# Splitting the experts' matrices in DVE's waits, a scan for the running sums, and earlier gathers at the end, in a one-core vision tower

## What is computed

```python
router_logits = jnp.einsum('bsh,he->bse', x, router_w) + router_b      # 8 experts
router_probs = jax.nn.softmax(router_logits, axis=-1)
top_k_probs, top_k_indices = jax.lax.top_k(router_probs, 2)
top_k_probs = top_k_probs / jnp.sum(top_k_probs, axis=-1, keepdims=True)
...
expert_out = jax.nn.gelu(jnp.einsum('bsh,ehd->ebsd', x, expert_w) + expert_b[:, None, None, :])
combined = jnp.einsum('bse,ebsd->bsd', gates, expert_out)
return jnp.einsum('bsd,df->bsf', combined, out_w) + out_b
...
h = h + _L0_ffn_ref(_layernorm(h, axis=-1), ...)
```

## Time and profile before

| | |
|---|---|
| median of 3 runs | 824.71 us (824.49 to 826.41) |
| the profiled execution | 825.01 us |
| its span in the trace | 823.2 us |
| PE busy | 699.2 us, 85% of the span |
| DVE busy | 537.3 us, 65% |
| ACT busy | 405.1 us, 49% |
| POOL busy | 157.6 us, 19% |
| PE's share of the chain that ended last | 64% |
| DVE's share of it | 22% |
| DMA's share of it | 6% |
| moved by DMA | 74.25 MB, 90 GB/s over the span |

### The profile page before, as it was taken

The page is one execution under the profiler, slowest core; times in us unless marked ns, Lnnn a source line. Parts: engine busy times, 40 slices in busy tenths (PEclk is TensorE's granted clock), DMA queues, the critical chain, the costliest instruction groups (busy, mean ns, idle before and its releaser), DMA issues.

```text
span 823.2 us, 16543 instructions
## 1 busy us (share of the span) xinstructions
PE 699.2 (85%) x5638; PEld 555.7 (68%) x5639; DVE 537.3 (65%) x1206; ACT 405.1 (49%) x1056; POOL 157.6 (19%) x282
## 2 busy tenths in 40 slices
PE   4758887879999999999999998775339999992998
PEld 3447877758787777868687785353328888881776
DVE  4998983657677777767677666457965444441765
ACT  4825544577576665757667565414623333330111
POOL 4000001000111102111111101124322323213451
PEclk9979999999999999999999999597559999996999
DMA  7100356200010000001000044142065566546774
GB/s 236 36 0 14 117 133 155 37 1 3 1 52 0 25 25 25 25 13 39 0 25 25 25 179 167 39 171 112 0 217 142 165 162 169 158 147 209 201 211 144
DMA packets 53495, 74.25 MB, mean 90 GB/s; under 512 B 24505, under 2 KB 26809, under 8 KB 53330
## 3 DMA queue, kind: packets, MB, share of 16 engines
q1 hardware_dynamic: 40338, 40.72, 15.2%
q0 software_dynamic: 5920, 19.40, 9.8%
q10 hardware_dynamic: 7200, 13.63, 4.3%
HBM read 45.42 MB, written 28.33 MB: 90 GB/s over the span
## 4 chain that ended last, share of the span: by engine, by line
PE 64%; DVE 22%; DMA 6%; issue 3%; ACT 3%; POOL 1%; SPq 0%; DVEq 0%; ACTq 0%; POOLq 0%
PE ps L1811 39%; PE ps L1914 7%; PE ps L1924 4%; PE ps L1907 4%; DMA rows<-y_slots,slot_of 4%; PE ps L2091 3%; DVE ring L1283 3%; DVE ring L1284 2%; PE ps L1956 2%; PE ps L1758 2%; DVE negmax L1351 2%; DVE ew_lo L1659 1%; DVE of_place L1639 1%; POOL rows L785 1%; DMA b_in<-in_L_tok_B_ri_dram 1%
## 5 line engine op out<-in xcount | busy, mean ns | idle before, releaser
L948 ACT ACTIVATE pts<-ps 128x512 f32<-128x512 f32 x128 | 77.2, 603 | 119.1 <-PE ps L1914 118.9
L940 ACT ACTIVATE prb<-ps,negmax 128x257 f32<-128x257 f32 x256 | 117.9, 479 | 4.5 <-DVE negmax L1351 3.5
L1351 DVE TENSOR_REDUCE negmax<-ps 128x2 f32<-128x514 f32 x128 | 82.5, 686 | 38.3 <-PE ps L1907 38.3
L1914 PE MATMUL ps<-ident,prb 128*128 128x128 f32 x512 | 84.4, 289 | 8.7 <-ACT pts L948 4.2
L1914 PEld LDWEIGHTS ps<-ident,prb 128*128 128x128 f32 x512 | 57.3, 144 | 33.9 <-issue 12.3
L1360 DVE TENSOR_SCALAR prb<-prb,rrec 128x258 f32<-128x258 f32 x256 | 73.4, 352 | 2.3
L1811 PE MATMUL ps<-ew_hi,xnT_hi 128*128 x160 | 66.9, 418 | 1.0 <-DVE xnT_lo L1549 1.0
L1086 ACT ACTIVATE rows<-ps 128x512 f32<-128x512 f32 x40 | 23.9, 598 | 87.7 <-DVE ps L1672 87.7
L1811 PE MATMUL ps<-ew_lo,xnT_hi 128*128 x160 | 63.6, 397 | 0.0
L1811 PE MATMUL ps<-ew_hi,xnT_lo 128*128 x160 | 63.6, 397 | 0.0
L1758 PE MATMUL ps<-ident,ring 128*128 128x128 f32 x384 | 48.2, 282 | 15.5 <-DVE ring L1284 14.4
(11 more groups left out here) (377 smaller groups left out, 1841.4 us busy)
## 6 DMA issues: line engine op xcount, KB each, us to landing
y_slots<-rows ACTq DMA_DIRECT2D x40, 256.0 KB
ew<-in_L_ffn_expert_w_dram SPq DMA_DIRECT2D x8, 1024.0 KB, 8.6
h_dram<-h_ob SPq DMA_DIRECT2D x17, 256.0 KB, 2.0
xn_dram<-tok SPq DMA_DIRECT2D x17, 256.0 KB, 2.2
h_early<-h_dram SPq DMA_DIRECT2D x9, 256.0 KB, 7.3
out_dram<-h_early SPq DMA_DIRECT2D x9, 256.0 KB
tok_dram<-so SPq DMA_DIRECT2D x4, 512.0 KB, 3.4
tok<-tok_dram SPq DMA_DIRECT2D x16, 128.0 KB, 3.0
```

The source lines that it names most:

```text
L940: e = act.activation(prb[:, u % 2, j, 0:KEYS], ps[:, j, 0:KEYS], ACT.Exp, bias=negmax[:, u % 2, j:j + 1], accum_out=rowsum[:, u % 2, j:j + 1])
L948: act.activation(pts[:, slot:slot + 2, :, st * P:(st + 1) * P], ps[:, 4, :].rearrange("p (h t s) -> p h t s", h=2, t=HALVES), ACT.Copy).th ...
L1351: dve.tensor_reduce(negmax[:, u % 2, 2 * b:2 * b + 2], ps[:, 2 * b:2 * b + 2, 0:KEYS], AX_X, ALU.max, negate=True).then_inc(s["dve_max"], 1)
L1914: mm = pe.transpose(ps[:, 4, (2 * j + tt) * P:(2 * j + tt + 1) * P], prb[:, u % 2, 2 * b + j, tt * P:(tt + 1) * P], ident[:, :])
```

## The change

- **Low parts.** POOL makes none. ACT makes the high parts of experts 0 to 2 at the end of attention, of 3 and 4 where 0 and 1 stood, 5 and 6 ahead of `of_tile`, and 7 behind it. DVE makes low parts 0 and 1 ahead of the last batch's first residual, 2 behind that residual's statistics, 3 ahead of reading the tokens' sums, 4 to 6 behind the gates and 7 behind the second slot tile's low part. PE waits, for the first two slot tiles, for the low part of the tile's own expert, and in the loop for all eight.
- **Running sums.** The table of picks is laid out by expert, then column. One scan with a table `inside` (1, and 0 where an expert's columns begin) gives the running sums and, in its last column, the row's count; L1605 and the six steps are gone.
- **Places.** `of_place` is made in four pieces (8, 8, 8 and 10 columns).
- **Output matrix.** Its load also waits for three turned slot tiles, ACT's high part follows the second gelu, and DVE's low part follows the last slot tile's low part. Two tiles of `h` are loaded ahead, the others one by one, each waiting for the combination of tile t - 2.
- **Gathers of the end.** DVE works out how many tiles of slots are used, rounded up to an even number; POOL loads the number and waits for so many stores only, and runs one small operation on `pairs_used` before it gathers. The ring has four tiles. Seven slot tiles that may stay unused are filled with zeros at startup, by seven stores of 256 KB on SP's queue. The first combinations wait for the last turned slot tile instead of the last expert matmul.

The diff, cut to its core:

```diff
             for k in range(SEL):
                 sp.dma_start(y_slots[(SLOTS + k) * P:(SLOTS + k + 1) * P, :], u_sb[:, :]).then_inc(st_h[k], 16)
+            for i in range(USED, SLOTS):
+                sp.dma_start(y_slots[i * P:(i + 1) * P, :], u_sb[:, :]).then_inc(ld_ew[NE - 1], 16)
...
             sp.wait_ge(s["dve_token_of"], 1)
+            sp.wait_ge(s["pe_slot_turned"], 3)
             sp.dma_start(ow[:, :, :], out_w.rearrange("(k p) d -> p k d", p=P)).then_inc(s["loaded_out_w"], 16)
             for t in range(EARLY_H):
-                sp.dma_start(h_early[:, t, :], h_dram[t]).then_inc(s["loaded_h"], 16)
+                sp.dma_start(of_end(t), h_dram[t]).then_inc(s["loaded_h"], 16)
             sp.wait_ge(s["pe_expert"], SLOTS)
-            for t in range(EARLY_H, NT):
-                sp.dma_start(h_late[:, t - EARLY_H, :], h_dram[t]).then_inc(s["loaded_h_late"], 16)
+            def load_h(t):
+                sp.wait_ge(s["dve_combined"], 2 * (t - 1))
+                sp.dma_start(of_end(t), h_dram[t]).then_inc(ld_ew[(t - EARLY_H) % Y_RING], 16)
+            load_h(EARLY_H)
             for t in range(TILES + 1):
+                if EARLY_H < t + 2 < NT:
+                    load_h(t + 2)
                 sp.wait_ge(s["dve_out"], t + 1)
...
-            for table in (chosen, cum_a, cum_b):
-                pool.memset(table[:, 0:PAD, :], 0.0).then_inc(s["pool_sums_cleared"], 1)
-            for e in range(POOL_LOWS):
-                pool.wait_ge(s["act_expert_high"], e + 1)
-                pool.tensor_tensor(ew_lo[:, e, :, :], ew[:, e, :, :], ew_hi[:, e, :, :].bitcast(F32), ALU.subtract
-                                   ).then_inc(s["pool_expert_low"], 1)
+            pool.memset(inside[:, :, :], 1.0).then_inc(s["pool_sums_cleared"], 1)
+            pool.wait_ge(s["pool_sums_cleared"], 2)
+            pool.memset(inside[:, :, 0], 0.0).then_inc(s["pool_sums_cleared"], 1)
...
+            pool.wait_ge(s["dve_stores_used"], 1)
+            stored = pool.value_load(stores_used[0:1, 0:1], min_val=8 * USED, max_val=8 * SLOTS)
             for done in st_y:
-                pool.wait_ge(done, 16 * SLOTS // 2)
+                pool.wait_ge(done, stored)
+            pool.tensor_tensor(pairs_used[:, 1:2], pairs_used[:, 0:1], pairs_used[:, 0:1], ALU.mult)
             for t in range(NT):
-                if t >= 2:
-                    pool.wait_ge(s["dve_combined"], 2 * (t - 1))
+                if t >= Y_RING:
+                    pool.wait_ge(s["dve_combined"], 2 * (t - Y_RING + 1))
...
             keep_pt(last, UNITS - 1, 0)
             keep_pt(last, UNITS - 1, 1)
+            act.wait_ge(s["pe_scores"], NB * UNITS)
+            act.wait_ge(s["pe_cls_scores"], NB)
+            act.wait_ge(s["pe_values"], NB * HALVES)
+            hi_expert(0)
             hi_ot(last, 3)
+            hi_expert(1)
+            act.wait_ge(s["pe_pv"], NB * KC)
+            hi_expert(2)
             act.wait_ge(s["dve_attn_done"], 1)
...
             gelu(1, 1, True)
+            act.wait_ge(s["loaded_out_w"], 16)
+            act.activation(ow_hi[:, :, :], ow[:, :, :], ACT.Copy).then_inc(s["act_out_w_high"], 1)
             with act.Fori(1, SLOTS // 2 - 1) as k:
...
+            for e in range(2):
+                lo_expert(e)
             residual(last, 0, 6)
             dve.wait_ge(s["dve_residual"], last * HALVES + 1)
             residual_stats(last, 0)
+            lo_expert(2)
             residual(last, 1, 7)
...
-            dve.tensor_reduce(row_count[:, :], picked.rearrange("p c e -> p e c"), AX_X, ALU.add
-                              ).then_inc(s["dve_row_count"], 1)
+            dve.tensor_tensor_scan(flat(cum), flat(inside), flat(picked), 0.0, ALU.mult, ALU.add
+                                   ).then_inc(s["dve_row_count"], 1)
             dve.tensor_tensor(spread[:, 0, :], top8[:, :, 1], top8[:, :, 0], ALU.subtract).then_inc(s["dve_gate_gap"], 1)
-            level, a, b = 1, chosen, cum_a
-            while level < COLS:
-                then(dve.tensor_tensor(b[:, PAD:, :], a[:, PAD:, :], a[:, PAD - level:PAD - level + COLS, :], ALU.add))
-                level, a, b = 2 * level, b, (cum_b if b is cum_a else cum_a)
...
+            then(dve.tensor_scalar(pairs_used[:, 0:1], tiles_to[:, 1, 3 + NE:4 + NE], 0.5, 0.25, ALU.mult, ALU.add))
+            then(dve.tensor_scalar(pairs_used[:, 1:2], pairs_used[:, 0:1], ROUND_MAGIC, ROUND_MAGIC, ALU.add, ALU.subtract))
+            dve.tensor_scalar(stores_used[:, :], pairs_used[:, 1:2], 16.0, None, ALU.mult).then_inc(s["dve_stores_used"], 1)
+            lo_expert(LOWS_IN_ATTENTION)
             dve.wait_ge(s["pe_token_of"], 1)
...
             lo_xs(1, 1)
+            lo_expert(NE - 1)
             dve.wait_ge(s["loaded_biases"], 16)
             add_bias(0, 0)
-            dve.wait_ge(s["act_out_w_high"], 1)
-            dve.tensor_tensor(ow_lo[:, :, :], ow[:, :, :], ow_hi[:, :, :].bitcast(F32), ALU.subtract
-                              ).then_inc(s["dve_out_w_low"], 1)
...
             def combine(t, u, first):
-                dve.wait_ge(got_y[u], 16 * (t - u) + 32)
+                dve.wait_ge(got_y[t % Y_RING], 32 * (t // Y_RING + 1))
                 if first:
-                    dve.wait_ge(s["pe_expert"], SLOTS)
+                    dve.wait_ge(s["pe_slot_turned"], SLOTS)
...
             def residual_out(t, u):
+                if t >= EARLY_H:
+                    dve.wait_ge(ld_ew[(t - EARLY_H) % Y_RING], 16 * ((t - EARLY_H) // Y_RING + 2))
...
             pe.wait_ge(s["dve_expert_of"], 1)
-            pe.wait_ge(s["dve_expert_low"], NE - POOL_LOWS)
-            pe.wait_ge(s["pool_expert_low"], POOL_LOWS)
```

More of the change, by code:

```diff
@@ L263, in vit_tower_kernel @@
         xnT_lo = sb(ffn, "xnT_lo", [P, 2, KC, P], F32R)
+        combT_hi, combT_lo, comb = xnT_hi, xnT_lo, rows[:, 0:2]
         eb = sb(ffn, "eb", [P, NE, D])
@@ L304, in vit_tower_kernel @@
             "pool_out_bias": "a tile with the output bias added, to be kept for the end",
-            "pool_sums_cleared": "zeros before the running sums",
-            "pool_expert_low": "low part of one of the first experts' matrices",
+            "pool_sums_cleared": "zeros ahead of the tiles' sums, then where the running sums of an expert begin",
             "act_exp_params": "exponentials of the parameters",
@@ L362, in vit_tower_kernel @@
             "dve_logits": "logits of four tiles with the bias",
-            "dve_row_count": "a row's number of entries for each expert",
+            "dve_row_count": "running sums of a row's entries for each expert",
             "dve_gate_gap": "second logits less first ones",
             "dve_hit": "the slots' tiles, one-hot",
-            "dve_onehot": "the slots' tiles times the tokens' tiles, then two pieces of the slots' places, one-hot",
+            "dve_onehot": "the slots' tiles times the tokens' tiles, then pieces of the slots' places, one-hot",
             "dve_token_of": "the token of every slot",
@@ L369, in vit_tower_kernel @@
             "dve_gates": "the gates",
+            "dve_stores_used": "how many stores of slots hold a token's result",
             "dve_expert_low": "low part of an expert's matrix",
@@ L422, in vit_tower_kernel @@
             "loaded_h": "the first token tiles, back for the end",
-            "loaded_h_late": "the other token tiles",
             "stored_xn": "normed token tiles",
@@ L593, in _ @@
                     sp.dma_start(out[:, 0, :], of_end(t)[0:NB]).then_inc(s["stored_out"], 16)
+            for done in st_y:
+                sp.wait_ge(done, 16 * SLOTS // 2)
             sp.wait_ge(s["stored_out"], (TILES + 1) * 16)
@@ L1063, in _ @@
                                ).then_inc(s["act_logitsT_kept"], 1)
-            for e in range(2):
+            for e in range(3, 5):
                 hi_expert(e)
@@ L1621, in _ @@
                                           in1=ps[:, 0, 0:NE], op0=ALU.mult, op1=ALU.add))
[L1622 to L1625 removed]
+            z = inside[:, :, :]
+            then(dve.tensor_tensor(z, cum[:, :, :], bc(first_slot[:, :].unsqueeze(2), [P, NE, COLS]), ALU.add))
+            then(dve.tensor_tensor(z, z, picked[:, :, :], ALU.mult))
+            then(dve.tensor_reduce(slotf[:, :], z.rearrange("p e c -> p c e"), AX_X, ALU.add))
             then(dve.tensor_tensor(slotf[:, COLS - SEL:], slotf[:, COLS - SEL:], spare[:, :], ALU.add))
@@ L1688, in _ @@
             lo_xs(SLOTS - 1, 1)
+            dve.wait_ge(s["act_out_w_high"], 1)
+            dve.tensor_tensor(ow_lo[:, :, :], ow[:, :, :], ow_hi[:, :, :].bitcast(F32), ALU.subtract
+                              ).then_inc(s["dve_out_w_low"], 1)
             add_bias(SLOTS - 2, 0)
@@ L2133, in _ @@
             pe.wait_ge(s["dve_row_count"], 1)
-            pe.matmul(ps[:, 0, 0:NE], before[:, :], row_count[:, :], start=True, stop=True)
-            pe.matmul(ps[:, 1, 0:NE], all_one[:, :], row_count[:, :], start=True, stop=True).then_inc(s["pe_ranks"], 1)
```

(11 more changed lines are left out.)

84 lines of the change are left out of this document (40 added, 44 removed).

## The result

| | before | after |
|---|---|---|
| median, runs side by side | 825.56 us (824.49 to 826.74) | 795.05 us (793.04 to 795.57) |
| the profiled execution | 825.01 us | 795.57 us |
| its span | 823.2 us | 793.6 us |

The ratio is 0.963 (95% interval 0.960 to 0.965): faster, by 30.5 us. The forecast was 791.4 with a range of 787.0 to 799.0. Its span would have been 789.6; the trace shows 793.6, so 4.0 us are to be found. Engine totals first, from the page of the kernel after: busy us and share of the span, then the engines' shares of the chain that ended last.

What follows compares the result with a forecast made beforehand. TensorE was busy 85% of the span, so time could only come from stretches where it waits. 16.2 us surviving to the last expert matmul plus 17.4 in the end stage, 33.6 off 825.01, gave 791.4; range 787.0 to 799.0.

Steps and rivals of the forecast that it cites:

- Routing, 12.0 off: Routing up to `token_of`: without POOL's low parts holding up DVE, `token_of` is there at 585.9 instead of 597.9.
- Low parts and first gathers, 18.4 in all: Between `token_of` and the experts: three low parts and the gathers nearly level, first expert matmul at 593.9 instead of 612.27.
- Attention tail, cost 0: Low parts 0 to 2 fit ACT's and DVE's holes at the end of attention: cost 0, at most 2.6 us.
- Nothing lost ahead of the routing: Startup stores of zeros and parts in attention taken at cost 0; routing starts as before, at 567.5.
- Output matrix, stall 2.2: Ahead of the fourth expert tile: later load and ACT's part stall PE, leaving 16.2 us off; stall bounds 0 to 4.
- Stores 0 to 35 and the meeting of gather and last bias: End stage: POOL waits for 36 tiles' stores; first gathered pair (743.1) meets DVE's last bias (743.06), old clock.
- First projection at the slow price, 5.1: Start of end stage: PE at its slow clock, projection 0 takes 5.1 us, 2.6 less at the fast level.
- Rival 2: PE keeps the 2.4 GHz level at the start of the end stage: 788.8 us, chance 0.20.
- PE sets the pace of the end: End stage: PE's turns and matmuls set 3.20 us a tile instead of 3.66; the stage is 17.4 off.
- rivals 1, 4, 5 and 6: Transfers pace end, 796.7 to 798.3 (0.20); 38 stores, 797.8 (0.05); routing stays long, 799.4 (0.04); transfers slower, 841 (0.03).
- 3: The attention tail or the startup isn't covered: 791.9 to 794.5 us, chance 0.08.

Runs made afterwards that it cites:

- Experiment 1: Changed kernel with POOL making low parts 0 to 2 in the routing again and DVE none in attention: 812.62 us, 13.3 above the changed kernel of its group.
- Experiment 3: Changed kernel with `of_place` in two pieces of 24 and 10 columns instead of four: 799.56 us, 0.3 above the changed kernel of its group.
- Experiment 2: Changed kernel with DVE making low parts 0 to 2 outside the attention tail, part 0 ahead of the tokens, others behind the gates: 806.98 us, 7.7 above its sibling.
- experiment 8: The changed kernel run again unchanged, as sibling of the last group's runs: 798.85 us, ratio 0.966 to the kernel before.
- 11: Changed kernel with the output matrix loaded in four parts and the seven stores of zeros moved later: 794.71 us, against 798.85 for the unchanged sibling.
- experiment 6: Changed kernel with each `h` tile of the end stage loaded a second time into an unused buffer (15 loads, 3.9 MB): 793.96 us, ratio 0.961.
- experiment 7: Changed kernel with ACT's high part of the output matrix eight slot tiles later and DVE's low part moved too, load unmoved: 793.82 us, ratio 0.960.
- Experiment 9: Also "the kernel with quarters": changed kernel, output matrix in four loads behind successive slot turns, `h` loads and ACT's and DVE's parts moved: 795.70 us, sibling 798.85.
- Experiment 4: Changed kernel with POOL waiting for the stores of all 40 slot tiles: 804.79 us, 10.8 above the 793.96 and 793.82 of its group.
- Experiments 5: Changed kernel with end-stage gathers only two tiles ahead instead of four: 800.01 us, 6.1 above the two fastest of its group.
- the three groups: The follow-up runs, each group on one chip beside the kernel before, which took 826.40, 826.75 and 826.48 us.

## Why the prediction was right, and where it was off

- **Routing, 12.0 off: right.** 18.3 us from the comparison to `token_of` (570.53 to 588.80), as forecast (18.36). Experiment 1 shows the reason by undoing it. One reading was loose: the second piece of `of_place` did not end with POOL's third subtraction (593.67) but 1.4 us behind it, at 595.04, its own length; the sum does not use it. The scan, taken at 0.64 between bounds of 0.44 and 2.7, took 0.73. PE was the bound behind the first piece, as said, and experiment 3 shows 2.1 us for the pieces at that place.
- **Low parts and first gathers, 18.4 in all: right to 0.1.** The two gathers and the three low parts were nearly level, as forecast: the gathers' turns wait until 592.89 and 594.84, DVE is free for the first slot low part at 595.91. Experiment 2 gives 6.7 us for three parts.
- **Attention tail, cost 0: right for this profile, and with less room than it seems.** Timeline of the kernel after; the last of these was forecast with its 0.65 beside POOL:

```profile
534.30 4.49 DVE L1543 TENSOR_TENSOR ew_lo<-ew,ew_hi 128x2048 fp32r<-128x2048 f32 x2
538.70 0.68 DVE L1390 TENSOR_TENSOR tok<-ps,tok 128x512 f32<-128x512 f32 x1
540.03 2.87 DVE L1543 TENSOR_TENSOR ew_lo<-ew,ew_hi 128x2048 fp32r<-128x2048 f32 x1
```

  The first residual stands 1.6 later than in the earlier trace rows, but it is not the parts that hold it: everything from 529 on is later by as much, and the chain runs through PE's matmuls there. The holes that the prediction measured were those of a PE at the slow level (the 16 matmuls ahead of `oT_hi` take 1.83 in the chain before and 1.97 after). In two later profiles, those of experiments 8 and 11, the same 16 take 1.08, at the full clock, and the chain goes through the moved parts instead. Chain of experiment 8:

```profile
529.76 1.36 ACT ew_hi L1047
...
533.85 4.40 DVE ew_lo L1543 x2
...
539.59 2.79 DVE ew_lo L1543
```

  ACT's part holds `oT_hi` from about 531.1 to 531.56 there, and DVE's hold the class rows' residual from about 543.9 to 544.28: some 0.8 us in all, an estimate from PE's last matmuls ahead of each (they end at 531.05 and 543.80).
- **Nothing lost ahead of the routing: wrong, by 3.0 in this profile, and for the most part not by the change.** 1.6 us had gathered by the end of attention, 0.3 of them already in a load ahead of every changed instruction (`b_in`, 8.00 against 7.70). The other 1.4 are a clock phase: behind the same wait of 3.35 us in both kernels, the 16 turns at 553.18 took 3.18 at the slow level. The next 16 took 1.90, the first ones of the kernel before 1.90, and those of experiment 6 as well. In the twelve other profiles, of this kernel and its variants, the comparison starts between 566.6 and 569.6, at 568.1 in the mean, where the kernel before has 567.5 and the kernel after 570.5: the profile after is the latest of all. The prediction took the trace of before as the common start of both sums and had no term for such phases; the range had to hold them, and did.
- **Output matrix, stall 2.2: mis-sized.** The time from the first to the fourth expert tile was 14.95 us against 14.55 (+0.4), but a term was missing: PE's clock behind the stop, +1.75. And the mechanism was only half of it. The step said issue to use, then ACT, then DVE; experiment 7 took ACT and DVE out and a stop of 1.98 stayed, because the loads issued beside it (1 MB of the matrix and 0.5 MB of `h`) also delay the fifth tile's gather. Experiment 9 spread them and the stop was gone.
- **Stores 0 to 35 and the meeting of gather and last bias: right, to 0.4.** The chain leads from the bias of tile 35 at 718.65 over its store to POOL at 724.00, and the first combination at 731.56 follows the last bias (730.95) without a wait; tile 1's waits 0.37. Experiment 4 prices the early start at 9 to 11 us.
- **First projection at the slow price, 5.1: mis-sized.** It took 3.86; the clock came back in its midst. Rival 2 took 2.6 off, so the truth lay between the two (in the terms of the chain, the kernel before had 4.82 for this projection, and a fast one takes 2.8). In experiment 7 it took 4.60, and in the kernel with quarters the whole first 10 us are slow. Which of these comes can't be read from the trace of before.
- **PE sets the pace of the end: right.** 3.23 a tile against 3.20, PE 20.00 of 20 us. Experiments 5 and 6 bound it on both sides: with two tiles of ring gathers pace it, with four there is room for 3.9 MB more. The likeliest case was the one that came; rivals 1, 4, 5 and 6 fell, 2 was half right, and 3 came closest to the time (791.9 to 794.5) with a reason that the runs don't bear out in this profile. That the total came within 3.7 us is in part luck: the slow clock behind the stop (+1.75) and the first projection (-1.6 with what is ahead of it) are errors of opposite sign, and on two other chips the same kernel took 799.

## What to carry to other kernels

Before moving elementwise work to GpSimd, look at what VectorE does at the same time: a POOL subtraction over 2048 elements made operations of 0.44 and 0.72 us take 4.7 to 4.9. Work placed in VectorE's own waits cost nothing while TensorE was the slower, and 0.8 us where TensorE happened to run at its full clock: measure such holes at both levels. A large load needed late is best cut into pieces, each behind one step of the loop, since it delays the small gathers beside it as well as its own consumer. A stop of 3 to 4 us cost TensorE more than its length (1.75 us on top in the kernel after, 2.7 in experiment 6), one of 2.0 did not. A DMA share near 1.0 is no proof of a limit: add a load and see whether the time moves.

## What the runs showed of the hardware that was not expected

- The DMA engines moved 407 GB/s of gathers, loads and stores over 20 us (experiment 6), above the 393 of the earlier trace rows; the share there reads 1.04 and was 0.98 at 339, so it does not tell what is left.
- A gather's issue on POOL takes 0.94 to 0.95 us alone. Beside DVE's low parts of the experts it took 1.25, 1.77 and 2.56 in the kernel after, and 2.12 beside the low part of `ow` (DVE, 727.50 to 729.78); in experiment 7, which has that part elsewhere, the same issue took 0.95.

```profile
594.25 2.56 POOL L781 DMA_INDIRECT rows<-xn_dram,token_of  x1 [1.82 <-PE ps L2112]
...
728.49 2.12 POOL L795 DMA_INDIRECT y_rows<-y_slots,slot_of  x1 [0.30 <-issue]
```

  The Trainium skill ("SBUF — State Buffer", "Who interferes with whom") excepts two-input operations from starving such issues, by inference; a low part has two inputs, and the longest issue beside one is 2.7 times as long as alone. The measurement decides.
- The kernel before gave the same time to 0.4 us on the chips of the three groups, while the changed one gave 799 on two, for the most part through one stop whose cause the trace doesn't name.
